# A fused attention and feed-forward kernel: the low parts of O are subtracted on POOL instead of VectorE

## The chip, the core and the metric

The kernel runs on one core of a Trainium2 chip. A core has a matrix engine (PE), VectorE (DVE), ScalarE (ACT), GpSimd (POOL) and a queue for transfers (SP). Each engine works through its own list of instructions in order; they wait for one another through semaphores. The metric is the device time of one execution in microseconds (us), lower is better.

## The reference

`x` has shape (2, 2048, 512). A conditioning layer first mixes `x` with a small vector. Its output goes through two layers of local attention and feed-forward, and the input is added at the end. Cut to one layer:

```python
h = shift_token(x)
q, k, v = split(h @ wqkv)                     # 8 heads of 64
q, k = l2norm(q) * q_scale, l2norm(k) * k_scale
q, k = rotary_xpos(q, k)
o = local_attention(q, k, v)                  # softmax over a band of 256 keys back, mask above
x = x + o @ wo
h = layernorm(shift_token(x)) * ln_g + ln_b
a, g = split(h @ w1 + b1)
x = x + (a * gelu(g)) @ w2 + b2
```

All arrays are float32. The kernel reaches this accuracy with a matrix engine format of less precision (fp32r): each operand is split into a high part, which is the value rounded to fp32r, and a low part, which is the value minus the high part. A product is three matmuls: high by high, low by high, high by low (`three_passes`, L343 to L345).

## The kernel before

The two sequences are 32 tiles of 128 rows. The stages follow one another: conditioning, attention of layer 0, its feed-forward, attention of layer 1, its feed-forward. The change is in the attention stage.

In attention each engine has a loop over steps t = -1 to 32, written out by hand; within a step its pieces belong to tiles t-1 (the end of attention), t (softmax and values), t+1 and t+2 (projections of q, k, v). The order in the code of each engine is the order of execution. Scores, probabilities and O of a tile are made for 8 heads, O in two halves g = 0 and 1 of four heads each.

What a tile x goes through:

- PE `k_project(x)` (L343 to L345, `a_wk`), ACT `square` and `k_copy` (L1004, L1012) to `a_sq` and `a_kraw`.
- POOL `rotate_k(x)`: three operations of 128x512, L1628, L1630, L1632, then `norms(1, x)`: 14 operations of 128x8, an inverse square root by Newton steps (L1597 to L1607), for k.
- DVE `k_norm(x)` (L1304) scales `a_krot`; PE transposes it (`k_T`, L578).
- POOL `rotate_q(x)`: L1617, L1619, L1621, and `norms(0, x)` for q, whose last operation writes `a_q8` (L1610). PE transposes `a_qrot` (`q_T`, L578). `a_q8` scales the scores in DVE's `mask_max` (L1339).
- ACT exponentials and normalization, PE transposes of the probabilities (`p_T`, L784), which ACT and DVE split (L1062, L1350), PE `pv` (L805).
- ACT and DVE add O up in `a_O`; ACT `o_hi(x, g)` rounds it (L1045, `a_OT_hi`), and `o_lo(x, g)` subtracts (L1365, `a_OT_lo`): 128x256, all operands in SBUF, on DVE.
- PE `project_out(x)` (L343 to L345 with `a_wo`) needs both halves of high and low.

PE's order in a step: `pv(t-1,1)`, `scores(t,1)`, `p_T(t,0)`, `v_project(t+1)`, `p_T(t,1)`, `k_T(t+1)`, `project_out(t-1)`, `q_T(t+1)`, `h_T(t+2)`, `pv(t,0)`, `scores(t+1,0)`, `p_T(t,2)`, `k_project(t+2)`, `p_T(t,3)`, `q_project(t+2)`. ACT gets k's projection right behind `k_project`, and `o_copy` of the next tile's half waits for `o_lo` of the last one.

Of the kernel before, what the change touches and what calls it, by code (L numbers as in the profile page):

```python
# [20 lines left out]
ALU = mybir.AluOpType  # L21
# [7 lines left out]
START = 1  # L29
# [29 lines left out]
def adaln_ffn_program(nc, x, cond, wqT, bq, wk, bk, wvT, bv, woT, bo,  # L59
# [49 lines left out]
    def pair(sb, name, shape):  # L109
        return sb(name + "_hi", shape, F32R), sb(name + "_lo", shape, F32R)  # L110

    with ctx:
# [38 lines left out]
        with ExitStack() as st:  # L151
# [5 lines left out]
            a_O = s("a_O", [P, PAIRS, P])  # L157
# [13 lines left out]
            a_OT = pair(s, "a_OT", [P, PAIRS, P])  # L171
# [103 lines left out]
        GROUPS = PAIRS // 2  # L275
# [24 lines left out]
        def here(x):  # L300

            return 0 <= x < TILES
# [890 lines left out]
        def _(dve):  # L1193
# [95 lines left out]
            def attention(l):  # L1289
                G = l * TILES  # L1290
                quarters = lambda ap: ap.rearrange("p (k n) -> p k n", k=4)

                def sums(which, x):

                    dve.wait_ge((a_q_squared, a_k_squared)[which], START + G + x + 1)
                    dve.wait_ge(a_norms_set, START + G + x)
                    dve.tensor_reduce(a_ss[:, which * H:(which + 1) * H], a_sq[:].rearrange("p (h d) -> p h d", d=HD),
                                      AX_X, ALU.add).then_inc(a_ss_set, 1)
# [44 lines left out]
                def inverse(x, i):  # L1343
                    dve.wait_ge(a_exp, START + (G + x) * H + 2 * i + 2)
                    dve.reciprocal(a_inv[:, x % 2, 2 * i:2 * i + 2], a_sum[:, x % 2, 2 * i:2 * i + 2]).then_inc(a_inv_set, 1)  # L1345
# [7 lines left out]
                def o_sum(x, g, odd):  # L1353

                    done = 2 * (GROUPS * (G + x) + g) + odd + 1
                    own = slice(odd * HD, odd * HD + HD)
                    total = a_O[own, 2 * g:2 * g + 2, :]
                    dve.wait_ge(a_O_copied, START + done)
                    dve.tensor_tensor(total, o_parts(odd)[0:HD, :, 1, :], total, ALU.add).then_inc(a_O_part, 1)
                    dve.wait_ge(a_O_part, START + done)  # L1360
                    dve.tensor_tensor(total, o_parts(odd)[HD:P, :, 0, :], total, ALU.add).then_inc(a_O_sum[odd], 1)

                def o_lo(x, g):
                    dve.wait_ge(a_O_hi, START + GROUPS * (G + x) + g + 1)
                    dve.tensor_tensor(a_OT[1][:, 2 * g:2 * g + 2, :], a_O[:, 2 * g:2 * g + 2, :], a_OT[0][:, 2 * g:2 * g + 2, :],  # L1365
                                      ALU.subtract).then_inc(a_O_lo, 1)

                def result(x):
                    dve.wait_ge(a_wo_mm, START + G + x + 1)
                    dve.wait_ge(a_res_in[x % 2], START + (l * (TILES // 2) + x // 2 + 1) * 16)  # L1370
                    dve.wait_ge(a_stored[x % 2], START + (l * (TILES // 2) + x // 2) * 16)
                    dve.tensor_tensor(out_tiles[:, x % 2, :], out_work[:], a_res[:, x % 2, :], ALU.add).then_inc(a_out_set, 1)
# [11 lines left out]
                def body():  # L1384
                    for t in STEPS:
                        if here(t + 1) and t >= 0:
                            sums(0, t + 1)
                        if here(t - 1):
                            o_sum(t - 1, 1, 0)
                            o_sum(t - 1, 1, 1)  # L1390
                        if here(t):
                            mask_max(t, 4)
                            mask_max(t, 5)
                            p_T(t, 0)
                        if here(t + 1):
                            k_norm(t + 1)
                        if here(t - 1):
                            o_lo(t - 1, 1)
                        if here(t):
                            mask_max(t, 6)  # L1400
                            inverse(t, 2)
                            mask_max(t, 7)
                            p_T(t, 1)
                        if here(t + 1):
                            value(t + 1)
                            k_T(t + 1)
                        if here(t - 1):
                            result(t - 1)
                        if here(t + 1):
                            q_T(t + 1)  # L1410
                        if here(t + 2) and t >= 0:
                            h_T(t + 2)
                        if here(t):
                            inverse(t, 3)
                            o_sum(t, 0, 0)
                            o_sum(t, 0, 1)
                        if here(t + 1):
                            mask_max(t + 1, 0)
                            mask_max(t + 1, 1)
                        if here(t):  # L1420
                            p_T(t, 2)
                        if here(t + 1):
                            mask_max(t + 1, 2)
                        if here(t + 2):
                            sums(1, t + 2)
                        if here(t + 1):
                            mask_max(t + 1, 3)
                            inverse(t + 1, 0)
                        if here(t):
                            p_T(t, 3)  # L1430
                        if here(t + 1):
                            inverse(t + 1, 1)
                        if here(t):
                            o_lo(t, 0)

                return Heads(head_h, head_k, head_q, body)

# [137 lines left out]
        def _(pool):  # L1575
            def attention(l):
                G = l * TILES
# [9 lines left out]
                def norms(which, x):  # L1587

                    base = (2 * (G + x) + 1 - which) * NORM_STEPS
                    own = slice(which * H, which * H + H)  # L1590
                    pool.wait_ge(a_ss_set, START + 2 * (G + x + 1) - which)
                    if which == 1:
                        pool.wait_ge(a_k_normed, START + G + x)
                    elif x >= 2:
                        pool.wait_ge(a_S_masked, START + (G + x - 1) * H)
                    waits_end(pool)
                    step(0, base, pool.tensor_scalar(a_ss[:, own], a_ss[:, own], 1e-24, None, ALU.max))  # L1597
                    waits_end(pool)

                    step(1, base, pool.tensor_scalar(a_rs[:, own].bitcast(I32), a_ss[:, own].bitcast(I32), -0.5, RSQRT_SEED,  # L1600
                                                     ALU.mult, ALU.add))
                    for i in range(3):
                        step(2 + 4 * i, base, pool.tensor_tensor(a_rt[:, own], a_rs[:, own], a_rs[:, own], ALU.mult))  # L1603
                        step(3 + 4 * i, base, pool.tensor_tensor(a_rt[:, own], a_rt[:, own], a_ss[:, own], ALU.mult))  # L1604
                        waits_end(pool)
                        step(4 + 4 * i, base, pool.tensor_scalar(a_rt[:, own], a_rt[:, own], -0.5, 1.5, ALU.mult, ALU.add))  # L1606
                        step(5 + 4 * i, base, pool.tensor_tensor(a_rs[:, own], a_rs[:, own], a_rt[:, own], ALU.mult))  # L1607
                    if which == 0:
                        waits_end(pool)
                        pool.tensor_scalar(a_q8[:, x % 2, :], a_rs[:, 0:H], -8.0, None, ALU.mult).then_inc(a_norms_set, 1)  # L1610

                def rotate_q(x):

                    pool.wait_ge(a_q_copied, START + G + x + 1)
                    pool.wait_ge(a_k_rotated, START + G + x + 1)
                    pool.wait_ge(a_QT_mm, START + G + x)
                    pool.tensor_tensor(halves(a_tmp[:]), halves(a_qraw[:])[:, :, ::-1, :], table(x, 1), ALU.mult)\  # L1617
                        .then_inc(a_qrot_step, 1)
                    pool.tensor_tensor(halves(a_qrot[:]), halves(a_qraw[:]), table(x, 0), ALU.mult).then_inc(a_qrot_step, 1)  # L1619
                    pool.wait_ge(a_qrot_step, START + 2 * (G + x) + 2)  # L1620
                    pool.tensor_tensor(a_qrot[:], a_qrot[:], a_tmp[:], ALU.add).then_inc(a_q_rotated, 1)  # L1621
# [50 lines left out]
                rotate_k(0)  # L1672
                norms(1, 0)
                for t in STEPS:
                    if here(t + 1):
                        rotate_q(t + 1)
                        norms(0, t + 1)
                    if t == -1:
                        clear_carry()
                    if here(t + 2):  # L1680
                        rotate_k(t + 2)
                        norms(1, t + 2)
# [58 lines left out]
```

## Time and profile before

| what | us |
|---|---|
| median of 3 runs | 3279.44 |
| lowest and highest | 3274.03, 3279.64 |
| profiled execution | 3281.98 |
| its span | 3279.8 |
| PE busy | 3108.5 (95%) |
| DVE busy | 1940.3 (59%) |
| ACT busy | 1513.4 (46%) |
| POOL busy | 1123.1 (34%) |

The attention stages lie at about 260 to 990 us and 1770 to 2500 us. The busy share of an engine is a mean over all stages. The chain that ended last is for 73% of the span on PE and for 14% on POOL. In a timeline a line gives the start, the duration, the engine, the line of the code and the tile it writes and reads; in brackets stands for how long the engine had been idle and what ended that.

### The profile page before, as it was taken

What the parts mean: (1) busy time and instruction counts of PE and PEld (TensorE: products, weight loads), DVE (VectorE), ACT (ScalarE), POOL (GpSimd) and SP (SyncE); (2) the same over time, 40 slices, a digit from 0 to 9 for tenths busy, and PEclk for the clock granted to TensorE, in tenths of its full rate; (3) what the DMA queues carried; (4) which work ended last, traced back from release to release, by engine and by line L of the source; (5) the groups of instructions that cost most, each with busy time, mean ns of one, the idle gap of its engine ahead of it and who ended that gap; (6) DMA issues with size and microseconds to landing.
All of it is one profiled execution on the core that took longest, in us unless ns stands there. A gap on an engine that the chain in (4) does not pass through costs nothing.

```text
span 3279.8 us, 49483 instructions
## 1 busy us (share of the span) xinstructions
PE 3108.5 (95%) x16534; PEld 2570.3 (78%) x16534; DVE 1940.3 (59%) x4061; ACT 1513.4 (46%) x3198; POOL 1123.1 (34%) x2438
## 2 busy tenths in 40 slices
PE   9997999999986999999998999999995999999999
PEld 8986888878765888888877788888874888887887
DVE  4655888888875333333323888888885443333332
ACT  1116888888872111111113888888883111111111
POOL 0316666666647000000035666666664200000000
PEclk8998999999987999999999999999996999999999
DMA  4420121111114111001131111111104211111110
GB/s 148 141 75 27 65 65 56 65 65 63 52 55 116 39 39 39 15 25 39 39 118 37 56 65 65 56 65 65 51 32 119 64 39 52 45 52 52 52 39 20
DMA packets 149789, 194.58 MB, mean 59 GB/s; under 512 B 23286, under 2 KB 90998, under 8 KB 149284
## 3 DMA queue, kind: packets, MB, share of 16 engines
q1 hardware_dynamic: 133700, 175.69, 16.5%
q10 hardware_dynamic: 15840, 15.73, 1.5%
q8 instruction: 137, 2.24, 0.3%
q14 instruction: 112, 0.92, 0.1%
HBM read 120.06 MB, written 41.95 MB: 49 GB/s over the span
## 4 chain that ended last, share of the span: by engine, by line
PE 73%; POOL 14%; issue 7%; DVE 3%; ACT 3%; POOLq 0%; DVEq 0%; SPq 0%; ACTq 0%
PE bank L343 21%; PE bank L345 20%; PE bank L344 20%; PE bank L578 3%; PE bank L805 3%; PE bank L769 3%; POOL a_krot L1632 2%; POOL a_tmp L1628 2%; POOL a_krot L1630 2%; PE bank L784 2%; POOL a_rt L1604 1%; POOL a_rs L1607 1%; POOL a_rt L1603 1%; DVE a_krot L1304 1%; POOL a_rt L1606 1%
## 5 line engine op out<-in xcount | busy, mean ns | idle before, releaser
L1161 ACT ACTIVATE f_gate<-bank,f_b 128x512 f32<-128x512 f32 (+1 forms) x176 | 121.4, 690 | 998.8 <-PE bank L345 998.8
L1510 DVE SCALAR_TENSOR_TENSOR f_uraw<-bank,f_b,f_gate 128x512 f32<-128x512 f32 (+1 forms) x176 | 132.1, 750 | 756.3 <-ACT f_gate L1161 756.2
L343 PE MATMUL bank<-f_hT_hi,f_w_hi 128*128 128x512 f32 (+1 forms) x1408 | 556.7, 395 | 15.6 <-ACT f_hT_hi L1142 14.2
L345 PE MATMUL bank<-f_hT_hi,f_w_lo 128*128 128x512 f32 (+1 forms) x1408 | 553.1, 393 | 0.0
L344 PE MATMUL bank<-f_hT_lo,f_w_hi 128*128 128x512 f32 (+1 forms) x1408 | 552.5, 392 | 0.0
L343 PEld LDWEIGHTS bank<-f_hT_hi,f_w_hi 128*128 128x128 f32 (+1 forms) x1408 | 261.0, 185 | 77.7 <-ACT f_hT_hi L1142 15.0
L1339 DVE CUSTOM_DVE_ANT_0 a_S<-bank,a_masks,a_q 128x384 f32<-128x384 f32 x512 | 302.4, 610 | 32.8 <-POOL a_q L1610 19.3
L1057 ACT ACTIVATE a_P<-a_S,a_bias 128x384 f32<-128x384 f32 x512 | 310.5, 612 | 11.9 <-DVE a_bias L1339 11.8
L345 PEld LDWEIGHTS bank<-f_hT_hi,f_w_lo 128*128 128x128 f32 (+1 forms) x1408 | 260.9, 185 | 64.4
L344 PEld LDWEIGHTS bank<-f_hT_lo,f_w_hi 128*128 128x128 f32 (+1 forms) x1408 | 261.1, 185 | 62.6
L1050 ACT ACTIVATE a_P<-a_P,a_inv 128x384 f32<-128x384 f32 x512 | 287.5, 611 | 46.0 <-DVE a_inv L1345 42.8
L343 PE MATMUL bank<-f_w_hi,f_u_hi 128*128 128x512 f32 (+1 forms) x704 | 277.9, 395 | 4.6 <-issue 4.6
L345 PE MATMUL bank<-f_w_hi,f_u_lo 128*128 128x512 f32 (+1 forms) x704 | 276.1, 392 | 0.0
L344 PE MATMUL bank<-f_w_lo,f_u_hi 128*128 128x512 f32 (+1 forms) x704 | 275.6, 391 | 0.0
L1350 DVE TENSOR_TENSOR a_PT<-bank,a_PT 128x768 fp32r<-128x768 f32 x256 | 242.8, 948 | 14.8 <-ACT a_PT L1062 14.8
L1643 POOL CAST a_wk_hi<-a_stage 128x512 fp32r<-128x512 f32 x8 | 4.6, 616 | 701.9 <-DMA a_stage<-in_L_ffn_wqkv 701.9
L1062 ACT ACTIVATE a_PT<-bank 128x768 fp32r<-128x768 f32 x256 | 208.2, 813 | 51.9 <-PE bank L784 41.0
L784 PE MATMUL bank<-ident,a_P 128*128 128x128 f32 x1536 | 217.6, 278 | 14.8 <-DVE a_PT L1350 14.8
L784 PEld LDWEIGHTS bank<-ident,a_P 128*128 128x128 f32 x1536 | 173.5, 141 | 65.1 <-issue 32.8
L805 PE MATMUL bank<-a_PT,a_V 128*128 128x256 f32 x1536 | 216.5, 292 | 7.8 <-issue 7.8
L805 PEld LDWEIGHTS bank<-a_PT,a_V 128*128 128x128 f32 x1536 | 203.0, 197 | 13.7 <-issue 8.6
L1514 DVE TENSOR_TENSOR f_u_lo<-f_uraw,f_u_hi 128x512 fp32r<-128x512 f32 (+1 forms) x176 | 125.2, 712 | 122.9 <-ACT f_u_hi L1165 122.9
(165 smaller groups left out, 6799.7 us busy)
## 6 DMA issues: line engine op xcount, KB each, us to landing
a_h<-x_layer_in SPq DMA_DIRECT2D x128, 128.0 KB, 2.2
a_res<-x_layer_in SPq DMA_DIRECT2D x64, 256.0 KB, 3.5
x_after_attention<-out_tiles SPq DMA_DIRECT2D x64, 256.0 KB, 2.7
f_res<-x_after_attention SPq DMA_DIRECT2D x64, 256.0 KB, 3.2
f_stage<-in_L_ffn_w SPq DMA_DIRECT2D x60, 256.0 KB, 3.5
a_V<-a_V SPq DMA_DIRECT2D x28, 512.0 KB, 5.1
f_h<-x_after_attention ACTq DMA_DIRECT2D x28, 512.0 KB, 4.2
c_x<-in_x SPq DMA_DIRECT2D x32, 256.0 KB, 3.1
```

The lines of the kernel that those rows point to most:

```text
L343: pe.matmul(dst, w[0], m[0], start=start, stop=False)
L344: pe.matmul(dst, w[0], m[1], start=False, stop=False)
L345: return pe.matmul(dst, w[1], m[0], start=False, stop=stop)
L784: mm = pe.transpose(pt_banks[:, odd, kb * P:(kb + 1) * P], a_P[:, (2 * i + odd) % 4, kb * P:(kb + 1) * P], ident[:])
L805: mm = pe.matmul(o_banks[odd][:, i * 2 * P:(i + 1) * 2 * P], a_V[:, x % QUAD + kb, 4 * g + 2 * i + odd, :, :].rearrange("p c d -> p (c d)" ...
L1050: act.activation(a_P[:, h % 4, :], a_P[:, h % 4, :], ACT.Copy, scale=a_inv[:, x % 2, h:h + 1])\
L1057: act.activation(a_P[:, h % 4, :], a_S[h % 2][:], ACT.Exp, bias=a_bias[:, h % 2:h % 2 + 1], scale=-1.0, accum_out=a_sum[:, x % 2, h:h + 1] ...
L1062: act.activation(a_PT[:, 2 * (i % 2):2 * (i % 2) + 2, :, 0, :], pt_banks[:, :, 0:WIN * P].rearrange("p h (k n) -> p h k n", k=WIN), ACT.Co ...
L1339: dve.tensor_tensor_reduce(a_S[b][:], score_bank(h)[:, 0:WIN * P], a_masks[:, min(x % TB, 2), :], a_q8[:, x % 2, h:h + 1], 3.0e38, ALU.add ...
L1350: dve.tensor_tensor(a_PT[:, r, :, 1, :], pt_banks[:, :, 0:WIN * P].rearrange("p h (k n) -> p h k n", k=WIN), a_PT[:, r, :, 0, :], ALU.subt ...
L1510: dve.scalar_tensor_tensor(f_uraw[0:ROWS[m], m % 2, :], bank[pair_of(u, m, end)][0:ROWS[m], :], f_b1[0:ROWS[m], 0, m:m + 1], f_gate[0:ROWS ...
L1514: dve.tensor_tensor(f_u[1][0:ROWS[m], m % 2, :], f_uraw[0:ROWS[m], m % 2, :], f_u[0][0:ROWS[m], m % 2, :], ALU.subtract).then_inc(f_u_lo, 1)
```

## The change

The two calls of `o_lo` leave DVE's loop, and the same subtraction is issued by POOL: `o_lo(t-1, 1)` at the head of a step, in front of `rotate_q(t+1)`, and `o_lo(t, 0)` behind `norms(0, t+1)`. Operands, sizes and the semaphores are the same.

```diff
@@ vector
-                def o_lo(x, g):
-                    dve.wait_ge(a_O_hi, START + GROUPS * (G + x) + g + 1)
-                    dve.tensor_tensor(a_OT[1][:, 2 * g:2 * g + 2, :], a_O[:, 2 * g:2 * g + 2, :], a_OT[0][:, 2 * g:2 * g + 2, :],
-                                      ALU.subtract).then_inc(a_O_lo, 1)
...
                         if here(t + 1):
                             k_norm(t + 1)
-                        if here(t - 1):
-                            o_lo(t - 1, 1)
                         if here(t):
                             mask_max(t, 6)
...
                         if here(t + 1):
                             inverse(t + 1, 1)
-                        if here(t):
-                            o_lo(t, 0)
@@ gpsimd
+                def o_lo(x, g):
+                    pool.wait_ge(a_O_hi, START + GROUPS * (G + x) + g + 1)
+                    pool.tensor_tensor(a_OT[1][:, 2 * g:2 * g + 2, :], a_O[:, 2 * g:2 * g + 2, :], a_OT[0][:, 2 * g:2 * g + 2, :],
+                                       ALU.subtract).then_inc(a_O_lo, 1)
...
                 for t in STEPS:
+                    if here(t - 1):
+                        o_lo(t - 1, 1)
                     if here(t + 1):
                         rotate_q(t + 1)
                         norms(0, t + 1)
+                    if here(t):
+                        o_lo(t, 0)
                     if t == -1:
                         clear_carry()
```

POOL at the head of a step, before: the end of k's norms, then q's rotation and the first operation of q's norms.

```order
L1604 TENSOR_TENSOR a_rt<-a_rt,a_ss 128x8
L1606 TENSOR_SCALAR a_rt<-a_rt 128x8
L1607 TENSOR_TENSOR a_rs<-a_rs,a_rt 128x8
L1617 TENSOR_TENSOR a_tmp<-a_qraw,a_rope 128x512
L1619 TENSOR_TENSOR a_qrot<-a_qraw,a_rope 128x512
L1621 TENSOR_TENSOR a_qrot<-a_qrot,a_tmp 128x512
L1597 TENSOR_SCALAR a_ss<-a_ss 128x8
```

The same place on POOL now. Line numbers of the changed program are smaller by 9 before `o_lo` and by 4 behind it.

```order
L1595 TENSOR_TENSOR a_rt<-a_rt,a_ss 128x8
L1597 TENSOR_SCALAR a_rt<-a_rt 128x8
L1598 TENSOR_TENSOR a_rs<-a_rs,a_rt 128x8
L1605 TENSOR_TENSOR a_OT_lo<-a_O,a_OT_hi 128x256
L1613 TENSOR_TENSOR a_tmp<-a_qraw,a_rope 128x512
L1615 TENSOR_TENSOR a_qrot<-a_qraw,a_rope 128x512
L1617 TENSOR_TENSOR a_qrot<-a_qrot,a_tmp 128x512
L1588 TENSOR_SCALAR a_ss<-a_ss 128x8
```

One instruction, `a_OT_lo`, has come between k's norms and q's rotation.

DVE around `k_norm`, before: the split of transposed probabilities, `k_norm`, `o_lo`, then the masks of heads 6 and 7 of tile t.

```order
L1350 TENSOR_TENSOR a_PT<-bank,a_PT 128x6x128
L1304 TENSOR_TENSOR a_krot<-a_krot,a_rs 128x512
L1365 TENSOR_TENSOR a_OT_lo<-a_O,a_OT_hi 128x256
L1339 ISA a_S,a_bias<-bank,a_masks,a_q 128x384
L1339 ISA a_bias 128x1
L1345 RECIPROCAL a_inv<-a_sum 128x2
```

The same place on DVE now.

```order
L1350 TENSOR_TENSOR a_PT<-bank,a_PT 128x6x128
L1304 TENSOR_TENSOR a_krot<-a_krot,a_rs 128x512
L1339 ISA a_S,a_bias<-bank,a_masks,a_q 128x384
L1339 ISA a_bias 128x1
L1345 RECIPROCAL a_inv<-a_sum 128x2
```

The masks follow `k_norm` directly. PE's list is unchanged.

## Rows read from the trace of the kernel before

**Rows 1.** page, part 1: busy us (share of the span) and instructions of each engine

```profile
PE 3108.5 (95%) x16534; PEld 2570.3 (78%) x16534; DVE 1940.3 (59%) x4061; ACT 1513.4 (46%) x3198; POOL 1123.1 (34%) x2438
```

**Rows 2.** busy us per engine, granted clock (1.00 full), DMA share, GB/s, in 250 us of attention

```profile
450.00:700.00 250.00, 239.81 (x1503) 201.40 (x1502) 216.70 (x479) 210.65 (x481) 164.19 (x401) 1.00 0.18 61
```

**Rows 3.** who waited for whom, 450 to 950 us: us in total, times, longest

```profile
PE bank L343 <- issue: 18.4, 23, 0.8
```

**Rows 4.** timeline of POOL: start us, us, operation, [idle before it <- what ended it]

```profile
625.81 1.30 POOL L1628 TENSOR_TENSOR a_tmp<-a_kraw,a_rope 128x512 f32<-128x512 f32 x1 [4.06 <-ACT a_kraw L1012]
628.44 1.35 POOL L1632 TENSOR_TENSOR a_krot<-a_krot,a_tmp 128x512 f32<-128x512 f32 x1
...
634.03 0.20 POOL L1607 TENSOR_TENSOR a_rs<-a_rs,a_rt 128x8 f32<-128x8 f32 x1
634.31 1.78 POOL L1617 TENSOR_TENSOR a_tmp<-a_qraw,a_rope 128x512 f32<-128x512 f32 x1
636.05 1.46 POOL L1619 TENSOR_TENSOR a_qrot<-a_qraw,a_rope 128x512 f32<-128x512 f32 x1
637.59 1.30 POOL L1621 TENSOR_TENSOR a_qrot<-a_qrot,a_tmp 128x512 f32<-128x512 f32 x1
...
643.52 0.24 POOL L1610 TENSOR_SCALAR a_q<-a_rs 128x8 f32<-128x8 f32 x1 [0.20 <-POOL a_rs L1607]
647.79 1.30 POOL L1628 TENSOR_TENSOR a_tmp<-a_kraw,a_rope 128x512 f32<-128x512 f32 x1 [4.03 <-ACT a_kraw L1012]
```

**Rows 5.** timeline of DVE in the same tile

```profile
627.73 0.92 DVE L1365 TENSOR_TENSOR a_OT_lo<-a_O,a_OT_hi 128x256 fp32r<-128x256 f32 x1
...
634.26 0.69 DVE L1304 TENSOR_TENSOR a_krot<-a_krot,a_rs 128x512 f32<-128x512 f32 x1 [0.54 <-POOL a_rs L1607]
634.87 1.50 DVE L1365 TENSOR_TENSOR a_OT_lo<-a_O,a_OT_hi 128x256 fp32r<-128x256 f32 x1
...
643.97 0.62 DVE L1339 CUSTOM_DVE_ANT_0 a_S<-bank,a_masks,a_q 128x384 f32<-128x384 f32 x1 [0.29 <-POOL a_q L1610]
645.05 0.95 DVE L1350 TENSOR_TENSOR a_PT<-bank,a_PT 128x768 fp32r<-128x768 f32 x1
```

**Rows 6.** timeline of PE (matmuls) in the same tile

```profile
635.01 0.66 PE L578 MATMUL bank<-ident,a_krot 128*128 128x128 f32 x4
636.47 0.47 PE L343 MATMUL bank<-a_wo_hi,a_OT_hi 128*128 128x512 f32 x1 [0.80 <-issue]
...
639.28 0.60 PE L578 MATMUL bank<-ident,a_qrot 128*128 128x128 f32 x4
639.72 0.60 PE L578 MATMUL bank<-ident,a_h 128*128 128x128 f32 x4
...
646.42 0.82 PE L784 MATMUL bank<-ident,a_P 128*128 128x128 f32 x6
```

**Rows 7.** timeline of PE's weight loads in the same tile

```profile
635.01 0.42 PEld L578 LDWEIGHTS bank<-ident,a_krot 128*128 128x128 f32 x4 [0.33 <-DVE a_krot L1304]
...
639.05 0.59 PEld L578 LDWEIGHTS bank<-ident,a_qrot 128*128 128x128 f32 x4
```

**Rows 8.** timeline of DVE at the first layer's end

```profile
982.96 0.42 DVE L1365 TENSOR_TENSOR a_OT_lo<-a_O,a_OT_hi 128x256 fp32r<-128x256 f32 x1 [0.54 <-ACT a_OT_hi L1045]
```

**Rows 9.** timeline of POOL in the first tile of layer 0

```profile
272.23 1.29 POOL L1628 TENSOR_TENSOR a_tmp<-a_kraw,a_rope 128x512 f32<-128x512 f32 x1 [8.30 <-ACT a_kraw L1012]
...
274.84 1.27 POOL L1632 TENSOR_TENSOR a_krot<-a_krot,a_tmp 128x512 f32<-128x512 f32 x1
...
280.62 1.78 POOL L1617 TENSOR_TENSOR a_tmp<-a_qraw,a_rope 128x512 f32<-128x512 f32 x1
...
283.72 1.26 POOL L1621 TENSOR_TENSOR a_qrot<-a_qrot,a_tmp 128x512 f32<-128x512 f32 x1
```

**Rows 10.** timeline of POOL behind attention: low parts of the feed-forward weights

```profile
990.91 2.50 POOL L1696 TENSOR_TENSOR f_w_lo<-f_stage,f_w_hi 128x512 fp32r<-128x512 f32 x2 [38.97 <-ACT f_w_hi L1133]
...
1048.67 1.67 POOL L1696 TENSOR_TENSOR f_w_lo<-f_stage,f_w_hi 128x340 fp32r<-128x340 f32 x2
```

## The prediction

> **What bounds the kernel now.** I read the busy shares first: PE is busy for 3108.5 of 3279.8 us, DVE for 59% and POOL for 34% [rows 1]. The change touches only the attention stages, so I took one stretch of steady attention: in 250 us PE is busy 239.81, DVE 216.70, POOL 164.19, at full granted clock [rows 2]. About one us in 23 of PE is left, so a change here can win only what PE now waits. The list of waits over 500 us of such work has for PE's own queue one entry of size: the matmuls of L343, 18.4 us in 23 tiles, 0.8 each, named "issue" [rows 3].
>
> The timeline of one tile shows what this is. A tile takes 22.0 us (k's rotation on POOL starts at 625.81 and again at 647.79 [rows 4]). It is one ring: k rotation on POOL, k norms (end 634.23), k_norm on DVE (634.26 to 634.95 [rows 5]), k's transposes on PE (635.01), project_out, q's transposes, ..., k_project, copy on ACT, and the next k rotation, for which POOL has waited 4.03 us [rows 4]. The 0.80 us hole lies between k's transposes and project_out (636.47) [rows 6], and at 634.87 to 636.37 DVE is in o_lo [rows 5], which project_out waits for. So the hole is o_lo's second half.
>
> The same rows show the second thing that matters: POOL ends q's rotation at 637.59 + 1.30 = 638.89 [rows 4], and PE loads the first weights of q's transposes at 639.05 [rows 7]. Only some 0.1 us lies between q's rotation and PE. POOL's idle 4 us stand elsewhere in the ring, not here.
>
> **Part 1: o_lo leaves VectorE.** 64 x 2 instructions go. What PE gets: project_out needs o_lo no longer than POOL takes, and could follow k's transposes without the hole, 0.80 us sooner. DVE's other work behind o_lo gets up to 1.4 us earlier, but PE shows no wait for it in the stretch up to q's transposes, so it is worth nothing by itself.
>
> What POOL gets: 1.50 us for a subtraction that takes 0.42 us where POOL is idle (982.96 us, layer's end [rows 8]) is waiting for POOL. The two engines shut each other out, in both directions: q's first multiplication takes 1.78 us beside k_norm, the same operation for k 1.30 us [rows 4]. The first tile, where DVE has no o_lo of the tile before, separates the two guests: q's rotation takes 280.62 to 284.98, 4.36 us, against 634.31 to 638.89, 4.58 us, in the steady state [rows 4, 9]. In it the first multiplication is still 1.78, so 0.49 us are k_norm's and 0.22 us were o_lo's. For k, the first tile needs 272.23 to 276.11, 3.88 us, against 625.81 to 629.79, 3.99 us [rows 4, 9]: the other o_lo cost 0.11 us there. That 0.11 us is on the ring and goes: the weight loads stand idle for 0.33 us ahead of k's transposes [rows 7], so k can come that much earlier.
>
> The Trainium skill (SBUF — State Buffer, Who interferes with whom) has this as an exclusive lock: a VectorE instruction with two SBUF inputs and a GpSimd one that reads SBUF hold the shared interface for the whole instruction, and the other waits. The trace agrees, 1.78 against 1.30 us. It speaks against the change in one way: the lock isn't avoided by moving o_lo, since k_norm still stands in front of whatever POOL does next.
>
> **Part 2: o_lo(t-1,1) on POOL, in front of q's rotation.** Sixty tiles (t = 1 to 30 in both layers) have a q rotation behind it. POOL has no row of a 128x256 subtraction. The nearest are the weight subtractions with fp32r output: 128x512 at 1.25 us each where unhindered (2.50 for two), 128x340 at 0.84 (1.67 for two) [rows 10]. The floor is half of the first, 0.63; the ceiling is the second whole, 0.84. With the 0.20 us that a 128x8 one takes [rows 4] as fixed part, the straight line to 1.25 gives 0.71; a line through the two large ones gives 0.63. I take 0.70, and 0.66 of it in a row, as independent POOL instructions follow each other 0.04 early (L1617 to L1619 [rows 4]).
>
> The Trainium skill (GPSIMD Engine Reference, 3.1) measures about 2.6 cycles per element for a two-input operation, at 1.2 GHz; by it alone the estimate is 0.55 us plus a fixed part, 0.75 us with a 0.20 one, and the sum below would be 3 us larger. No run here shows that operation yet.
>
> Now the chain. The k norms end at 634.23 as before. o_lo starts at 634.31 where L1617 did, 0.05 behind k_norm, and takes over its 0.49 us of waiting. Then 0.66, then the rotation undisturbed, 3.88: 634.31 + 0.49 + 0.66 + 3.88 = 639.34, 0.45 later than now. PE meanwhile is through with project_out 0.8 us earlier and now waits for q: start 639.34 + 0.06 = 639.40. A start after a wait takes 0.66 us for the four transposes (k's at 635.01), a running one 0.60 (639.28, next work 0.44 behind) [rows 6]; so h's transposes, next in PE's order, start at 639.40 + 0.50 = 639.90 instead of 639.72: +0.18 us. Less the 0.11 of k's path: +0.07 us per tile. The hole has moved, not gone.
>
> Its ends: o_lo at 0.63 gives 0.00, at 0.84 +0.21 per tile, 0 to +13 us for 60 tiles. An o_lo that cost nothing at all would give -0.6 per tile.
>
> **Part 3: o_lo(t,0) on POOL behind q's norms.** a_q8 ends at 643.76 [rows 4], 0.45 later then; o_lo and its wait for ACT's high part end about 646, and POOL is idle until 647.79 [rows 4]. Free: the cover is those 4.03 us, of which 2.5 remain. At the end of each layer the last half (0.42 us on DVE [rows 8]) is on the path; on POOL it is 0.7: 2 x 0.3 = 0.6 us.
>
> **Part 4: q's norms come 0.45 later.** DVE's mask_max for the next tile waits 0.29 for a_q8 already (643.97), and its p_T at 645.05 to 646.0 [rows 5] is what PE's p_T (loaded 0.2 ahead of 646.42 [rows 6]) waits for. With +0.45 on DVE and +0.18 on PE the two meet within 0.1 us. k_project is issued ahead of it, so the ring isn't hit; the spare 0.3 us ahead of k's transposes takes it. I price it at 0, with up to +0.15 per tile if I am wrong.
>
> **Sum.** 60 x 0.07 + 0.6 = 4.8 us. Against the profiled execution's own 3281.98 us this is 3286.8; that execution lies 2.5 above the median of the runs, 3279.44, so I forecast 3284.
>
> **The rivals.**
> First, the hole closes for good (faster). For it: PE waited 18.4 us in 23 tiles on exactly this, and DVE loses 2.4 us of work a tile. It needs q's rotation not to bind, for instance if o_lo on POOL hides in the time for which k_norm holds POOL up anyway. Half of the limit, -0.3 per tile: -18, 3262; all of it, -36, 3244. Against it: only 0.1 us between q's rotation and PE's load.
> Second, the masks bind (slower): part 4 at +0.15 on top, +9: 3293.
> Third, the port changes hands (slower). If POOL's o_lo took the lock before k_norm, k_norm would wait 0.66, and if q's first multiplication, which follows o_lo without a gap, took it again, 1.3 more. k's transposes would start some 2 us later and q's, behind 2.8 us of project_out, 1.1 us later than now: +66, 3350. It decides once o_lo starts ahead of k_norm. Against it: k_norm starts 0.05 us before POOL's next instruction [rows 4, 5], and that one takes 1.78 us in the first tile as in the steady state [rows 4, 9].
> Fourth, o_lo near its ceiling (with layout or wait overhead), +13: 3293; this is the upper part of my own case.
>
> **Chances.** My case (the hole moves to q's transposes, 0 to +13 us) 0.62; the hole closes at least in part 0.16; masks 0.15; port 0.07. A difference under 0.2%, 6.6 us or 0.11 us per tile, can't be told from none. Of my case 0.42 lie within it, 0.18 above, 0.02 below. So faster 0.18, within 0.2% 0.45 (with a little of the masks), slower 0.37. The likeliest case alone spans 3277 to 3293; the range for 8 in 10 reaches into both sides, 3264 to 3300.
>
> **What would show it.** PE's idle ahead of L343 at project_out gone, and in its place about 0.4 to 0.5 us ahead of q's transposes, with POOL's q rotation as what ended it. The first POOL instruction behind the k norms, o_lo, at about 1.2 us, the other o_lo at 0.7; q's first multiplication back to 1.29, k_norm unchanged at 0.69. The period of a tile 22.0 to 22.2. I am wrong if the period falls below 21.9 or PE doesn't wait ahead of q's transposes.

## The result, and the profile after

The changed kernel takes 3290.15 us (median of 6 runs, 3288.88 to 3293.33), the one before 3278.56 us (6 runs, 3274.03 to 3279.84): a ratio of 1.004, with a 95% interval of 1.0027 to 1.0053. It is slower by 0.4%, 11.6 us. The profiled executions have spans of 3290.8 and 3279.8 us.

Busy times of the engines, and the chain that ended last, from the page of the changed kernel:

```profile
PE 3122.6 (95%) x16534; PEld 2563.2 (78%) x16534; DVE 1807.0 (55%) x3933; ACT 1507.4 (46%) x3198; POOL 1200.9 (36%) x2566
...
PE 66%; POOL 23%; issue 7%; ACT 2%; DVE 1%; POOLq 0%; DVEq 0%; SPq 0%; ACTq 0%
```

DVE lost 133 us of busy time, POOL gained 78, and the kernel became slower [rows 1]. The chain tells where to look: POOL's share of it went from 14% to 23%.

The same 250 us of steady attention as in [rows 2], with the same columns:

```profile
450.00:700.00 250.00, 240.89 (x1497) 198.46 (x1496) 190.82 (x455) 208.01 (x478) 176.38 (x420) 1.00 0.19 61
```

Who waited for whom from 450 to 950 us of the changed kernel (us in total, times, longest):

```profile
PEld bank L578 <- POOL a_qrot L1617: 27.6, 22, 1.3
...
PE bank L578 <- POOL a_qrot L1617: 18.4, 22, 0.9
```

The 0.8 us that PE lost at project_out, [rows 3], are gone from the list of PE's matmuls. In their place PE's matmuls wait 0.8 us, 22 times, for `a_qrot`, and the weight loads 1.3 us.

One tile on POOL, beside [rows 4] (L1624 to L1628 is k's rotation, L1605 o_lo, L1613 to L1617 q's rotation, L1601 the last of q's norms):

```profile
626.55 1.30 POOL L1624 TENSOR_TENSOR a_tmp<-a_kraw,a_rope 128x512 f32<-128x512 f32 x1 [1.99 <-ACT a_kraw L1012]
...
629.18 1.29 POOL L1628 TENSOR_TENSOR a_krot<-a_krot,a_tmp 128x512 f32<-128x512 f32 x1
...
634.71 0.20 POOL L1598 TENSOR_TENSOR a_rs<-a_rs,a_rt 128x8 f32<-128x8 f32 x1
634.99 1.24 POOL L1605 TENSOR_TENSOR a_OT_lo<-a_O,a_OT_hi 128x256 fp32r<-128x256 f32 x1
636.19 1.29 POOL L1613 TENSOR_TENSOR a_tmp<-a_qraw,a_rope 128x512 f32<-128x512 f32 x1
...
638.81 1.28 POOL L1617 TENSOR_TENSOR a_qrot<-a_qrot,a_tmp 128x512 f32<-128x512 f32 x1
...
644.72 0.24 POOL L1601 TENSOR_SCALAR a_q<-a_rs 128x8 f32<-128x8 f32 x1 [0.20 <-POOL a_rs L1598]
645.95 0.74 POOL L1605 TENSOR_TENSOR a_OT_lo<-a_O,a_OT_hi 128x256 fp32r<-128x256 f32 x1 [0.99 <-ACT a_OT_hi L1045]
648.68 1.30 POOL L1624 TENSOR_TENSOR a_tmp<-a_kraw,a_rope 128x512 f32<-128x512 f32 x1 [1.99 <-ACT a_kraw L1012]
```

DVE's k_norm and PE in the same tile, beside [rows 5, 6]:

```profile
634.94 0.69 DVE L1304 TENSOR_TENSOR a_krot<-a_krot,a_rs 128x512 f32<-128x512 f32 x1 [0.47 <-POOL a_rs L1598]
```

```profile
635.69 0.66 PE L578 MATMUL bank<-ident,a_krot 128*128 128x128 f32 x4
636.33 0.47 PE L343 MATMUL bank<-a_wo_hi,a_OT_hi 128*128 128x512 f32 x1
...
640.14 0.66 PE L578 MATMUL bank<-ident,a_qrot 128*128 128x128 f32 x4 [0.82 <-POOL a_qrot L1617]
640.63 0.60 PE L578 MATMUL bank<-ident,a_h 128*128 128x128 f32 x4
```

From k rotation to k rotation it is 648.68 - 626.55 = 22.13 us. Over the last 29 intervals of a layer the median is 22.13 and 22.14 us, against 21.99 and 21.98 before, and but for one interval in layer 1 (22.43) each lies within 0.04 of it. The first o_lo of the step takes 1.24 us and the second, of the same shape, 0.74: the first one starts 0.05 us behind k_norm. project_out follows k's transposes at 636.33 with no hole, and then PE is idle for 0.82 us until 640.14, 0.05 us after POOL has finished `a_qrot` (638.81 + 1.28). POOL's idle time ahead of k's rotation is 1.99 us, where it was 4.03.

Over the whole span: the 29 steady intervals of the two layers add 3.9 and 4.5 us, 8.5 together. The other 3.0 lie at the ends of the layers. From the last k rotation through the last q norm to the last result of layer 0, in the kernel before:

```profile
934.01 1.30 POOL L1628 TENSOR_TENSOR a_tmp<-a_kraw,a_rope 128x512 f32<-128x512 f32 x1 [4.05 <-ACT a_kraw L1012]
...
951.71 0.24 POOL L1610 TENSOR_SCALAR a_q<-a_rs 128x8 f32<-128x8 f32 x1 [0.20 <-POOL a_rs L1607]
```

```profile
988.12 0.69 DVE L1372 TENSOR_TENSOR out_tiles<-bank,a_res 128x512 f32<-128x512 f32 x1 [4.74 <-PE bank L345]
```

and in the changed one:

```profile
936.46 1.30 POOL L1624 TENSOR_TENSOR a_tmp<-a_kraw,a_rope 128x512 f32<-128x512 f32 x1 [1.99 <-ACT a_kraw L1012]
...
954.63 0.24 POOL L1601 TENSOR_SCALAR a_q<-a_rs 128x8 f32<-128x8 f32 x1 [0.19 <-POOL a_rs L1598]
```

```profile
992.14 0.69 DVE L1367 TENSOR_TENSOR out_tiles<-bank,a_res 128x512 f32<-128x512 f32 x1 [6.90 <-PE bank L345]
```

54.1 us became 55.7 us, and in layer 1 54.2 became 55.7. `a_q8` is there 18.2 us behind the start of k's rotation instead of 17.7, and the last o_lo takes 0.72 us instead of 0.42. But most of the 1.5 us is the same work of PE at a lower clock. PE often waits at a layer's end (2.78 us ahead of the last project_out), and its granted clock changes there between its two levels (1.2 and 2.4 GHz). The last project_out, 12 matmuls, takes 4.56 us before and 5.41 us changed; busy times and granted clock in these stretches are, before and changed:

```profile
983.50:988.10 4.60, 4.56 (x12) 3.38 (x12) 0.00 (x0) 0.00 (x0) 0.00 (x0) 0.63 0.00 0
```

```profile
986.70:992.10 5.40, 5.40 (x12) 3.77 (x12) 0.00 (x0) 0.00 (x0) 0.00 (x0) 0.52 0.00 0
```

The last transposes of probabilities take 1.18 us instead of 0.85 as well. These two make 1.18 of layer 0's 1.57 us, and the last o_lo 0.30. The delay of `a_q8`, 0.47 us, is down to 0.06 where the values matmuls (`pv`) begin at 972.93 (36.47 us behind k's rotation, against 36.41 before). The remaining -0.5 us of the whole difference are in the starts of the layers and the feed-forward stages.

### The profile page after: what moved, and what is told of

It is laid out like the page before. It is cut to its first block, busy times and chain, and to the rows that moved or that the text cites. A ratio compares the mean times of both kernels' runs of the same rounds, so it can differ in the third digit from the quotient of the medians.

```text
span 3290.8 us, 49483 instructions
## 1 busy us (share of the span) xinstructions
PE 3122.6 (95%) x16534; PEld 2563.2 (78%) x16534; DVE 1807.0 (55%) x3933; ACT 1507.4 (46%) x3198; POOL 1200.9 (36%) x2566
## 4 chain that ended last, share of the span: by engine, by line
PE 66%; POOL 23%; issue 7%; ACT 2%; DVE 1%; POOLq 0%; DVEq 0%; SPq 0%; ACTq 0%
PE bank L343 18%; PE bank L345 18%; PE bank L344 18%; PE bank L805 3%; PE bank L578 3%; PE bank L769 3%; POOL a_tmp L1624 2%; POOL a_krot L1628 2%; POOL a_tmp L1613 2%; POOL a_qrot L1617 2%; POOL a_qrot L1615 2%; POOL a_krot L1626 2%; POOL a_OT_lo L1605 2%; PE bank L784 2%; POOL a_rt L1595 1%
```

## The experiments

Each changes a few lines of the kernel before or of the changed one. "Period" is the median distance of k's rotations in a layer, read from one profiled execution. Each ratio is against runs of the kernel before that were made together with the experiment (medians of 3275.15 to 3276.62 us).

**Which half costs: half1_only.** Only the second half goes to POOL.

```diff
 # gpsimd, kernel before
 for t in STEPS:
+    if here(t - 1):
+        o_lo(t - 1, 1)
     if here(t + 1):
         rotate_q(t + 1)
 # vector
-    if here(t - 1):
-        o_lo(t - 1, 1)
```

> Only o_lo(t-1,1) goes to POOL, in front of q's rotation; o_lo(t,0) stays on DVE. Theory (the period is set by k norms, o_lo, q's rotation, q's transposes): the whole loss is here, and the k rotation keeps its o_lo on DVE, which costs it 0.06 us; period 22.14 + 0.06 = 22.20 us, 0.2 more than before, about 3293 us. Rival (the loss comes from q's norms and masks being late, or from POOL having two more instructions in all): half of the loss, 3284. Rival (the half behind q's norms is what costs): period below 21.99, faster than before.

Measured 3290.83 us, ratio 1.0045 (1.003 to 1.006), period 22.18 us. POOL in one tile:

```profile
606.19 1.30 POOL L1631 TENSOR_TENSOR a_tmp<-a_kraw,a_rope 128x512 f32<-128x512 f32 x1 [3.75 <-ACT a_kraw L1012]
...
608.83 1.35 POOL L1635 TENSOR_TENSOR a_krot<-a_krot,a_tmp 128x512 f32<-128x512 f32 x1
...
614.68 1.23 POOL L1612 TENSOR_TENSOR a_OT_lo<-a_O,a_OT_hi 128x256 fp32r<-128x256 f32 x1
```

and one line of its list of waits:

```profile
PE bank L578 <- POOL a_qrot L1624: 18.3, 22, 0.9
```

The k rotation keeps its 1.35 us operation, o_lo takes 1.23 us, and PE's wait for `a_qrot` is the same as in the changed kernel. The whole loss is in this half.

**Which half costs: half0_only.** Only the first half goes to POOL.

```diff
 # gpsimd, kernel before
         norms(0, t + 1)
+    if here(t):
+        o_lo(t, 0)
 # vector
-    if here(t):
-        o_lo(t, 0)
```

> Only o_lo(t,0) goes to POOL, behind q's norms; the other half stays on DVE behind k_norm. Theory: the k rotation sheds the 0.06 us that this o_lo costs it and nothing on the ring comes later; period 21.93 us instead of 21.99, hole of 0.8 us at project_out unchanged, about 3275 us. Rival (any o_lo on POOL delays k's rotation): period above 22.0, slower than before.

Measured 3275.28 us, ratio 0.9995 (0.9986 to 1.0005), no difference that the times can tell; the period, 21.90 us in both layers, is 0.09 us shorter than before. POOL's k rotation, and PE's hole, which stays:

```profile
601.41 1.30 POOL L1631 TENSOR_TENSOR a_tmp<-a_kraw,a_rope 128x512 f32<-128x512 f32 x1 [1.99 <-ACT a_kraw L1012]
...
604.05 1.29 POOL L1635 TENSOR_TENSOR a_krot<-a_krot,a_tmp 128x512 f32<-128x512 f32 x1
```

```profile
PE bank L343 <- issue: 18.5, 23, 0.8
```

L1635 (k's last operation) takes 1.29 us instead of 1.35. The k rotation as a whole is 0.06 us shorter; where the other 0.03 us of the step come from I did not find.

**Late rotation or late norms: dummy_front and dummy_behind.** The same extra subtraction, whose result nobody uses, on POOL in 58 tiles. Each of the two kernels has one of the two call lines at the end of the diff.

```diff
 # gpsimd, kernel before
+def dummy(x):
+    if 1 <= x < TILES - 2:
+        pool.wait_ge(a_dummy, START + l * (TILES - 3) + x - 1)
+        pool.tensor_tensor(a_stage[0][:, 0, 0:2 * P], a_rope[:, 0, :, :]..., a_rope[:, 1, :, :]..., ALU.subtract).then_inc(a_dummy, 1)
...
+        dummy(t + 1)       # dummy_front
         rotate_q(t + 1)
+        dummy(t + 1)       # dummy_behind
         norms(0, t + 1)
```

> The kernel before, with one extra subtraction of 128x256 on POOL in front of q's rotation in 58 tiles; its result is used by nobody. Both o_lo stay on DVE. Theory (q's rotation is on the ring): it ends about 0.7 us later, q's transposes wait for it; k's path keeps its 3.99 us; period 22.2 to 22.4 us against 21.99, 3288 to 3300 us. Rival (what cost time was the late q norms and masks): the same period as dummy_behind.

> The same extra subtraction, between q's rotation and q's norms. The rotation is as early as before, a_q8 is 0.7 us later, which is more than the 0.47 of the changed kernel. Theory: the masks have room, period 21.99 to 22.05 us, 3277 to 3281 us. Rival (late masks hold up the transposes of the probabilities and so PE): period 22.15 or more, 3287 and above.

In front: 3299.79 us, ratio 1.0076 (1.0061 to 1.0091), period 22.37. Behind: 3277.08 us, ratio 1.0007 (0.9998 to 1.0016), period 21.98 and 21.99. POOL in dummy_front (L1615 is the extra one, L1623 to L1627 q's rotation):

```profile
607.22 1.30 POOL L1634 TENSOR_TENSOR a_tmp<-a_kraw,a_rope 128x512 f32<-128x512 f32 x1 [3.75 <-ACT a_kraw L1012]
...
615.73 1.23 POOL L1615 TENSOR_TENSOR a_stage<-a_rope 128x256 f32<-128x256 f32 x1
616.93 1.47 POOL L1623 TENSOR_TENSOR a_tmp<-a_qraw,a_rope 128x512 f32<-128x512 f32 x1
...
619.73 1.28 POOL L1627 TENSOR_TENSOR a_qrot<-a_qrot,a_tmp 128x512 f32<-128x512 f32 x1
...
629.61 1.30 POOL L1634 TENSOR_TENSOR a_tmp<-a_kraw,a_rope 128x512 f32<-128x512 f32 x1 [3.74 <-ACT a_kraw L1012]
```

Two lines of the waits of dummy_behind:

```profile
DVE a_S L1339 <- POOL a_q L1610: 20.9, 22, 1.2
...
PE bank L343 <- issue: 15.3, 23, 0.8
```

DVE waits for `a_q8` 0.95 us a tile there (20.9 in 22), three times as long as before [rows 5], and nothing is lost. Late norms are free in the steady state; a late rotation is paid. That dummy_front costs more than the changed kernel (22.37 against 22.14) fits as well: both o_lo are still on DVE in it, and q's first multiplication takes 1.47 us there instead of 1.29.

**Taking o_lo out of the ring altogether: dve_first.** On DVE, in front of k_norm instead of behind it.

```diff
 # vector, kernel before
+if here(t - 1):
+    o_lo(t - 1, 1)
 if here(t + 1):
     k_norm(t + 1)
-if here(t - 1):
-    o_lo(t - 1, 1)
```

> Both o_lo stay on DVE; o_lo(t-1,1) goes in front of k_norm instead of behind it. Theory: POOL then has only q's rotation (4.36 us with k_norm's 0.49 us of waiting) between the k norms and q's transposes, and the hole at project_out is gone; q's transposes come 0.5 us earlier than before, less what o_lo takes from POOL's k norms (0 to 0.4 us): period 21.5 to 21.9 us, 3250 to 3273 us. PE should then wait about 0.4 us ahead of q's transposes. Rival (PE is full anyway and the hole is no loss): 3279. Rival (o_lo delays k_norm and with it k's transposes): slower, 3290.

Measured 3257.07 us, ratio 0.9945 (0.993 to 0.9959), period 21.69 and 21.70. One tile on DVE, POOL and PE:

```profile
625.54 0.41 DVE L1365 TENSOR_TENSOR a_OT_lo<-a_O,a_OT_hi 128x256 fp32r<-128x256 f32 x1
626.33 0.69 DVE L1304 TENSOR_TENSOR a_krot<-a_krot,a_rs 128x512 f32<-128x512 f32 x1 [0.38 <-POOL a_rs L1607]
```

```profile
617.70 1.31 POOL L1628 TENSOR_TENSOR a_tmp<-a_kraw,a_rope 128x512 f32<-128x512 f32 x1 [3.75 <-ACT a_kraw L1012]
...
625.64 0.37 POOL L1606 TENSOR_SCALAR a_rt<-a_rt 128x8 f32<-128x8 f32 x1 [0.20 <-POOL a_rt L1604]
...
626.38 1.80 POOL L1617 TENSOR_TENSOR a_tmp<-a_qraw,a_rope 128x512 f32<-128x512 f32 x1
628.13 1.30 POOL L1619 TENSOR_TENSOR a_qrot<-a_qraw,a_rope 128x512 f32<-128x512 f32 x1
...
639.40 1.30 POOL L1628 TENSOR_TENSOR a_tmp<-a_kraw,a_rope 128x512 f32<-128x512 f32 x1 [3.74 <-ACT a_kraw L1012]
```

```profile
627.08 0.66 PE L578 MATMUL bank<-ident,a_krot 128*128 128x128 f32 x4 [0.22 <-DVE a_krot L1304]
...
630.86 0.66 PE L578 MATMUL bank<-ident,a_qrot 128*128 128x128 f32 x4 [0.37 <-POOL a_qrot L1621]
```

o_lo fits into the half microsecond that DVE waited for k's norms [rows 5] and takes 0.41 us instead of 1.50. POOL's operations beside it are 0.2 us long, and it stretches one of them to 0.37. q's second multiplication is back from 1.46 to 1.30. PE's hole of 0.80 is gone and a smaller one, 0.37, stands ahead of q's transposes.

**The two together: dve_first_pool0.** dve_first with the first half on POOL as in half0_only.

> As dve_first (o_lo(t-1,1) on DVE in front of k_norm), and o_lo(t,0) on POOL behind q's norms. Theory: the two gains add up, 0.06 us per tile on top of dve_first, 4 us less than it: 3246 to 3269 us. Rival (POOL's second instruction costs): not faster than dve_first.

Measured 3259.68 us, ratio 0.9951 (0.9936 to 0.9965), period 21.70: no gain over dve_first. My expectation that the gains add up was wrong. The k rotation does get shorter, 3.92 us against 3.99 in dve_first, but k's norms behind it then meet o_lo at a worse moment. One tile on DVE and POOL:

```profile
629.14 0.41 DVE L1365 TENSOR_TENSOR a_OT_lo<-a_O,a_OT_hi 128x256 fp32r<-128x256 f32 x1
```

```profile
629.15 0.46 POOL L1604 TENSOR_SCALAR a_rt<-a_rt 128x8 f32<-128x8 f32 x1 [0.20 <-POOL a_rt L1602]
```

The norm operation starts just behind o_lo and takes 0.46 us. In dve_first the same operation starts 0.10 us behind it and takes 0.37. Over 52 steady tiles the medians are 0.46 and 0.39, so the 0.07 us are lost again: k_norm starts 8.64 us behind k's rotation in the one and 8.63 in the other.

**Filling the wait: after_h_first and dve_first_h.** h's transposes stand in front of q's, on PE, ACT and DVE.

```diff
 # tensor, scalar and vector alike
-if here(t + 1):
-    q_T(t + 1)
 if here(t + 2) and t >= 0:
     h_T(t + 2)
+if here(t + 1):
+    q_T(t + 1)
```

> The changed kernel with h's transposes (and their copies on ACT and DVE) in front of q's. Theory: PE waits some 0.8 us for q's rotation there; h's four transposes, 0.44 us apart, fill that time, and the values part behind them starts 0.4 us earlier; ACT and DVE get q's part no later. Period 22.14 - 0.4 = 21.75 us, 3267 us. Rival (PE is bound elsewhere, the wait is no loss): 22.14, 3290.

> dve_first (o_lo(t-1,1) on DVE in front of k_norm) with h's transposes in front of q's. Theory: the 0.37 us that PE waits for q's rotation in dve_first is filled by h's transposes: period 21.70 - 0.35 = 21.35 us, 3236 us, unless PE's own work of a tile binds first. Rival (the chain from q's transposes over ACT and DVE to the scores binds): 21.70, 3257.

after_h_first: 3268.54 us, ratio 0.9981 (0.9972 to 0.9991), period 21.80. dve_first_h: 3246.0 us, ratio 0.991 (0.9894 to 0.9927), period 21.43. PE in after_h_first:

```profile
633.98 0.60 PE L578 MATMUL bank<-ident,a_h 128*128 128x128 f32 x4
634.96 0.66 PE L578 MATMUL bank<-ident,a_qrot 128*128 128x128 f32 x4 [0.38 <-POOL a_qrot L1617]
```

The wait for `a_qrot` fell from 0.82 to 0.38 us, the 0.44 that four transposes take. q's transposes start as late in the step as in the changed kernel (13.6 us behind k's rotation, median), but k_project starts 17.60 us behind it instead of 17.93. So the wait was on the path: filled with work that was due anyway, 0.34 us of it came back per tile, and the changed kernel became faster than the one before. The same order of transposes in the kernel before, without another change, was not run.

**The ends of the layers: after_tail_dve.** The changed kernel with the last five o_lo of a layer at their old places on DVE.

```diff
+def late(x, g):
+    return 2 * x + g >= 2 * (TILES - 3) + 1
...
-    if here(t - 1):
+    if here(t - 1) and not late(t - 1, 1):
         o_lo(t - 1, 1)        # gpsimd; the same for o_lo(t, 0), and the opposite on vector
```

> The changed kernel, but from the second half of tile 29 on the last five o_lo of each layer are back on DVE, at their old places; all earlier ones stay on POOL. Theory (at a layer's end the path runs through q's norms of tile 31 and through the last o_lo, so each layer's end is 1.5 us longer in the changed kernel): the way from the last k rotation to the last result is 54.1 to 54.3 us again, against 55.7; the period stays 22.14; 3 us less than the changed kernel, 3287 us. Rival (the ends differ by chance or by PE's clock): 55.7 again, 3290.

Measured 3285.62 us, ratio 1.0034 (1.0021 to 1.0048); period 22.12 and 22.13. The end of layer 0 on POOL and DVE:

```profile
938.96 1.30 POOL L1637 TENSOR_TENSOR a_tmp<-a_kraw,a_rope 128x512 f32<-128x512 f32 x1 [1.99 <-ACT a_kraw L1016]
...
956.57 0.24 POOL L1614 TENSOR_SCALAR a_q<-a_rs 128x8 f32<-128x8 f32 x1 [0.20 <-POOL a_rs L1611]
```

```profile
987.77 0.42 DVE L1369 TENSOR_TENSOR a_OT_lo<-a_O,a_OT_hi 128x256 fp32r<-128x256 f32 x1 [0.54 <-ACT a_OT_hi L1049]
992.91 0.69 DVE L1376 TENSOR_TENSOR out_tiles<-bank,a_res 128x512 f32<-128x512 f32 x1 [4.71 <-PE bank L349]
```

From the last k rotation to the last result it is 53.95 us (before 54.11, changed 55.68), in layer 1 53.45. `a_q8` comes 17.6 us behind k's rotation again. That is what I had expected, but it doesn't show that the place of these five instructions sets the length of the end. The traces of the other runs speak against it (us; the first column is the start of the last `a_q8` and the last column that of the last result, both counted from the start of the last k rotation):

| kernel, layer | `a_q8` | last o_lo | last project_out | last result |
|---|---|---|---|---|
| before, 0 | 17.70 | 0.42, DVE | 4.56 | 54.11 |
| changed, 0 | 18.17 | 0.72, POOL | 5.41 | 55.68 |
| after_tail_dve, 0 | 17.61 | 0.42, DVE | 4.52 | 53.95 |
| half1_only, 0 | 18.17 | 0.72, POOL | 4.36 | 51.84 |
| half1_only, 1 | 18.23 | 0.72, POOL | 4.37 | 55.42 |
| half0_only, 0 | 17.62 | 0.42, DVE | 5.46 | 54.80 |
| half0_only, 1 | 17.66 | 0.43, DVE | 4.36 | 53.52 |

half1_only has the late `a_q8` and the last o_lo on POOL, and in layer 0 its end is 2.3 us shorter than before. half0_only has neither, and in layer 0 its end is longer than before. The two layers of one program differ by up to 3.6 us. From 20 us behind the last k rotation to the last result the mean granted clock is 0.79 in the shortest of these ends (half1_only, layer 0), 0.70 before and 0.66 in the changed kernel. So of the changed kernel's longer end PE's clock, the rival that I had named, has the larger part, and of the rest 0.30 us come from the last o_lo being on POOL. Whether their place also moves the clock isn't shown. Nor is a gain in time: the intervals of this run and of the changed kernel (1.0027 to 1.0053) overlap.

**The best version: both_moves_h.** dve_first_h with the first half on POOL.

> dve_first_h with o_lo(t,0) on POOL behind q's norms. Theory: in dve_first_h PE is busy for 247.5 of 250 us, so the 0.06 us that k's rotation sheds can bring 0 to 0.06 per tile: period 21.38 to 21.44 us, 3242 to 3246 us. Rival (o_lo on POOL delays k's rotation): above 21.5, 3250.

Measured 3241.11 us, ratio 0.9894 (0.9878 to 0.9911), period 21.36 and 21.37: 1.1% faster than the kernel before and the lowest median of all, though its interval overlaps with that of dve_first_h. Here the first half on POOL does shorten the period (21.43 and 21.44 to 21.36 and 21.37). In 250 us:

```profile
450.00:700.00 250.00, 247.39 (x1551) 206.06 (x1548) 203.14 (x483) 215.65 (x489) 175.85 (x429) 1.00 0.20 64
```

PE is busy 247.4 of 250 us; little waiting is left to remove.

| kernel | us | ratio | period |
|---|---|---|---|
| changed | 3290.15 | 1.004 | 22.14 |
| half1_only | 3290.83 | 1.0045 | 22.18 |
| half0_only | 3275.28 | 0.9995 | 21.90 |
| dummy_front | 3299.79 | 1.0076 | 22.37 |
| dummy_behind | 3277.08 | 1.0007 | 21.99 |
| dve_first | 3257.07 | 0.9945 | 21.70 |
| dve_first_pool0 | 3259.68 | 0.9951 | 21.70 |
| after_h_first | 3268.54 | 0.9981 | 21.80 |
| dve_first_h | 3246.0 | 0.991 | 21.43 |
| after_tail_dve | 3285.62 | 1.0034 | 22.13 |
| both_moves_h | 3241.11 | 0.9894 | 21.36 |

## Why the prediction was right, and where it was short

The mechanism was the forecast one: the hole moves to q's transposes. The time, 3290, lies in the range of 3264 to 3300 and in the likeliest case's own, 3277 to 3293. The forecast figure of 3284 was 6 us low: I had added 4.8 us, and the kernel lost 11.6. I gave "within 0.2%" the largest chance, 0.45, while the kernel became slower by 0.4%. Step by step:

- **The hole closes, and PE waits for q instead** (parts 1 and 2): right. The list of signs gave the wait as 0.4 to 0.5 us, and it is 0.82. That figure didn't follow from my own sum, by which PE was ready at 639.28 - 0.80 = 638.48 and started at 639.40, 0.92 later; the sum itself used the start, so it isn't touched.
- **k_norm's 0.49 us pass to o_lo**: right, 1.24 against 0.74 us, and q's first multiplication is back to 1.29. half1_only shows the same with that half alone.
- **o_lo at 0.70 us on POOL**: it takes 0.74. The estimate from the 2.6 cycles per element of the Trainium skill (GPSIMD Engine Reference, 3.1), 0.75 us with a fixed 0.20, was nearer to it than my line through two rows.
- **The rotation undisturbed at 3.88 us, and k's path 0.11 us shorter**: both a little off, for one reason. I took the undisturbed rotation from the first tile (by the trace it is the second: its k rotation follows one at 242.64). In the steady state it takes 3.90 us (636.19 to 640.09), and k's path became shorter by only 0.06 (634.91 - 626.55 = 8.36, against 634.23 - 625.81 = 8.42 [rows 4]).
- **The start of PE behind the wait**: right, 0.05 us behind POOL, 0.66 us for four transposes, h's 0.49 behind q's start.
- Together these make the mis-sized term: forecast +0.07 us per tile, measured +0.15, or 8.5 us where the sum has 4.2. k's path has 0.05 us of the 0.08, o_lo 0.04 and the rotation 0.02; the rest of the step is some 0.02 shorter.
- **o_lo(t,0) behind q's norms is free** (part 3): right in the steady state; half0_only is 0.09 us shorter per tile. I wrote that 2.5 us of POOL's idle time would remain, but my own figures give 647.79 - 646 = 1.8, and 1.99 remained. The last o_lo of a layer costs 0.30 us more, as priced.
- **Late norms cost nothing** (part 4): right in the steady state, as dummy_behind shows with more delay. At the ends the sum has 0.3 us per layer, and each grew by 1.5 us. The sum has no term for PE's clock there: the same last project_out took 0.85 us longer in layer 0. How much of that belongs to the change isn't shown: with the same late `a_q8` and last o_lo an end also came out 2.3 us shorter than before (half1_only, layer 0). What the late `a_q8` costs at an end can't be told apart from it.
- **The rivals**: the closed hole didn't come, as it needs a rotation that isn't late; dve_first is that case, and gains 0.29 us per tile, what I had priced as half of the limit. The late masks aren't what costs in the steady state (dummy_behind). The port did not change hands: k_norm takes 0.69 us as before.

## What to carry to other kernels

A wait of 0.8 us that can be named is worth only what lies between it and the next wait behind it: read how early the next operand is there before moving anything in front of its producer. When two engines shut each other out, place an operation beside the other engine's short operations, and in a time in which its own engine waits; here that alone turned 1.50 us into 0.41 and made the kernel 0.5% faster, where the move to POOL made it 0.4% slower. And before a difference at the end of a stage is put down to a moved instruction, compare PE's granted clock there, and the same stretch in the other layer and in other runs: here the end of a layer varied from 51.8 to 55.7 us, and one run that came out as expected looked like a proof.

## What I had not expected

The 128x256 subtraction costs DVE 1.50, 0.92 or 0.41 us, by what POOL does at that moment, while its operands have the same sizes and types. And the gain of the first half on POOL depends on the rest: 0.09 us per tile from the kernel before, nothing on top of dve_first, 0.07 on top of dve_first_h. And the end of a layer differs by up to 3.6 us between the two layers of one program.
